# One in sixteen of layer 1's differences on VectorE instead of GpSimd

## What is computed

```
h = relu(layernorm(x));  x = x + layer0(h, adj)     # additive attention over all nodes, 8 heads of 64
h = relu(layernorm(x));  x = x + layer1(h, adj)

def layer1(h, adj):
    keys, queries, values = h @ Wk[head], h @ Wq[head], h @ Wv[head]      # 8 heads of 64
    atts = queries @ keys.T / 8 - 1e16 * (1 - max(adj, eye))
    return sum over heads of softmax(atts) @ values @ Wo[head]
```

## Time and profile before

| | before |
|---|---|
| median of 3 runs | 4598.18 us (4594.34 to 4601.94) |
| the profiled execution | 4598.45 us |
| span of its trace | 4596.6 us |
| busy, share of the span | TensorE 94%, VectorE 80%, GpSimd 75%, ScalarE 71% |
| mean granted clock of TensorE | 0.976 of full |
| DMA | 646.10 MB, mean 141 GB/s |

### The profile page before, as it was taken

How to read it: one execution, slowest core, us unless ns; L and a number is a source line. 1 busy time by engine, 2 the same in 40 slices (tenths; PEclk the granted TensorE clock), 3 DMA queues, 4 the chain that set the end, 5 groups by cost and what they waited for, 6 DMA issues and landing times. The chain is left out here.

```text
span 4596.6 us, 111803 instructions
## 1 busy us (share of the span) xinstructions
PE 4336.9 (94%) x42445; PEld 2092.0 (46%) x42956; DVE 3684.9 (80%) x7790; ACT 3250.4 (71%) x6022; POOL 3426.1 (75%) x2955
## 2 busy tenths in 40 slices
PE   8699999999999979969999999999999999999998
PEld 4222222222222224425665656656656566566565
DVE  5498998988989863358888888878888888888786
ACT  5366666666666643317888878888878788888886
POOL 2476676676767730018998989989989899899897
PEclk9899999999999989979999999999999999999999
DMA  4566676666666533362343433433433334334333
GB/s 145 136 212 195 204 216 211 212 206 212 221 188 204 151 126 115 115 193 75 105 123 88 123 98 96 135 107 98 120 105 113 106 89 127 110 99 129 98 111 104
DMA packets 462939, 646.10 MB, mean 141 GB/s; under 512 B 49536, under 2 KB 271104, under 8 KB 452288
## 3 DMA queue, kind: packets, MB, share of 16 engines
q1 hardware_dynamic: 383968, 522.36, 37.1%
q10 hardware_dynamic: 73856, 100.83, 7.7%
q0 software_dynamic: 4576, 15.73, 1.2%
HBM read 528.38 MB, written 110.38 MB: 139 GB/s over the span
## 5 line engine op out<-in xcount | busy, mean ns | idle before, releaser
L1406 POOL TENSOR_TENSOR d_PL<-d_PF,d_PH 128x512 f16<-128x512 f32 x2048 | 2316.1, 1170 | 234.9 <-ACT d_PH L1456 230.6
L1496 DVE CUSTOM_DVE_ANT_0 d_junk<-d_gd,d_MR 128x512 bf16<-128x512 f32 x2112 | 1438.7, 687 | 412.0 <-issue 342.3
L1452 ACT ACTIVATE d_PF<-d_sc 128x512 f32<-128x512 f32 x2048 | 1253.8, 612 | 445.9 <-DVE d_sc L1585 297.3
L813 DVE SCALAR_TENSOR_TENSOR b_P<-R,u,b_A 128x512 f32<-128x512 f32 x1792 | 1195.2, 738 | 110.8 <-PE b_den L871 68.5
L1456 ACT ACTIVATE d_PH<-d_sc 128x512 f16<-128x512 f32 x2048 | 1262.3, 616 | 0.0
L864 PE MATMUL b_acc<-b_P,V 128*64 128x512 f32 x4096 | 965.4, 610 | 76.0 <-DVE b_P L813 38.4
L1624 PE MATMUL d_gd<-d_KA,d_QA 128*128 128x512 f16 x2112 | 816.1, 387 | 74.3 <-DMA d_KA<-scratch_kl 30.2
L1640 PE MATMUL d_sc<-d_QA,d_KA 128*128 128x512 f16 x2048 | 777.1, 379 | 13.9 <-ACT d_PH L1456 5.4
L1641 PE MATMUL d_sc<-d_QL,d_KB 128*128 128x512 f16 x2048 | 776.6, 379 | 0.0
L1661 PE MATMUL d_acc<-d_V,d_PH 128*128 128x65 f16 x8192 | 639.5, 193 | 2.7 <-ACT d_PH L1456 0.2
L1663 PE MATMUL d_acc<-d_V,d_PH 128*128 128x64 f16 x8192 | 640.3, 193 | 0.0
(11 more groups left out here) (133 smaller groups left out, 4075.8 us busy)
## 6 DMA issues: line engine op xcount, KB each, us to landing
d_V<-scratch_v SPq DMA_DIRECT2D x131, 520.0 KB, 4.2
stage<-in_adjT SPq DMA_DIRECT2D x128, 512.0 KB, 5.2
b_srow<-in_adj ACTq DMA_DIRECT2D x256, 256.0 KB, 4.3
b_rows<-in_adj SPq DMA_DIRECT2D x112, 512.0 KB, 6.4
d_MR<-scratch_mr SPq DMA_DIRECT2D x36, 1024.0 KB, 6.3
d_MT<-scratch_mt SPq DMA_DIRECT2D x35, 1024.0 KB, 6.3
d_KA<-scratch_kh SPq DMA_DIRECT2D x272, 128.0 KB, 3.0
d_KA<-scratch_kl SPq DMA_DIRECT2D x272, 128.0 KB, 3.2
```

Source lines behind the costliest of these rows:

```text
L813: nc.vector.scalar_tensor_tensor(out=PT[:, m % P_STEPS, h, :], in0=R[:, par, h, :], scalar=T["u"][:, m, h:h + 1], in1=A[m % A_RING][:, :], ...
L1406: eng.tensor_tensor(PL[:, t % H_RING, :], PF[:, t % F_RING, :], PH[:, t % H_RING, :], ALU.subtract).then_inc(s_lowp if by_pool(t) else s_l ...
L1452: nc.scalar.activation(PF[:, t % F_RING, :], sc[(nb * TILES + t) % BANKS][:, :], ACT.Exp, scale=EXP_SCALE)
L1496: nc.vector.tensor_tensor_reduce(out=junk[:, gi % 2, :], in0=gd[gi % 2][:, :], in1=MR[:, s, c * QB:(c + 1) * QB], scale=1.0, scalar=-3.0e3 ...
```

## The change

`by_pool(t)` is now true for all tiles but those with t % 16 == 2. These, 16 in a block and 128 in all, are subtracted by VectorE, in the place in its order that `body` has for them: at the start of the step after the tile's own, after `finish` and ahead of the step's first guard. In a pass they are the tiles of steps 1, 9, 17 and 25, so VectorE does them in steps 2, 10, 18 and 26. The slots of `PF` and the engines no longer go together, so the waits are written by tile: ScalarE, before tile t, waits for the difference of tile t - 4 on the engine that makes it, and TensorE for that of tile t. The first values of the two semaphores are 0 instead of the ring's shares.

```diff
-    POOL_SLOTS = (0, 1, 2, 3)
-    PER_RING = (F_RING - len(POOL_SLOTS), len(POOL_SLOTS))
-    SPLITS = tuple(n * TILES // F_RING for n in PER_RING)
...
     def by_pool(t):
-        return t % F_RING in POOL_SLOTS
+        return t % 16 != 2
+
+    SPLITS = tuple(sum(by_pool(t) == own for t in range(TILES)) for own in (False, True))
...
+    def splits_done(nb, t):
+
+        return nb * SPLITS[by_pool(t)] + split_count(t)
...
-            pool.sem_inc(s_lowp, PER_RING[1])
...
-                            act.wait_ge(s_lowp if by_pool(t) else s_low, nb * SPLITS[by_pool(t)] + split_count(t))
+                            if t >= F_RING:
+                                act.wait_ge(s_lowp if by_pool(t - F_RING) else s_low, splits_done(nb, t - F_RING))
+                            elif not first:
+                                before = t - F_RING + TILES
+                                act.wait_ge(s_lowp if by_pool(before) else s_low, splits_done(nb - 1, before))
...
-            if PER_RING[0]:
-                dve.sem_inc(s_low, PER_RING[0])
...
-                    own = by_pool(t)
-                    pe.wait_ge(s_lowp if own else s_low, nb * SPLITS[own] + (PER_RING[own] + split_count(t)))
+                    pe.wait_ge(s_lowp if by_pool(t) else s_low, splits_done(nb, t))
```

## The result

| | before | after |
|---|---|---|
| median (7 runs each) | 4598.70 us (4594.34 to 4604.85) | 4611.87 us (4607.34 to 4613.38) |
| ratio, 95% interval | | 1.0024 [1.0014, 1.0035] |
| profiled execution, its span | 4598.45, 4596.6 | 4609.6, 4607.7 |

A forecast was written before the change was run, and what follows sets the result against it. The prediction took TensorE to set the pace, with GpSimd next. Its terms, 3.0 + 3.8 + 6.4 = 13.2 us, added to 4598 gave 4611 us, 0.28% slower, range 4588 to 4626 (the forecast's own 4607 to 4618).

The forecast's parts named there:

- TensorE sets the pace, GpSimd's relief is worth nothing: Layer 1's attention: TensorE busy 294.6 of 300 us, so taking 128 instructions off GpSimd gains about nothing.
- Rival D: GpSimd was the limit after all and 6% less of its work counts: 4553 us; chance 0.02.
- The bare price of a split: One difference on VectorE, without a wait for GpSimd, delays its next instruction by 0.61 us.
- Steps 10, 18 and 26: Three of four splits in a pass: VectorE's delay is absorbed, cost 0 for 96 splits.
- Rival C's full form: A GpSimd difference has just begun at every split, shutting VectorE out, in steps 10, 18, 26 too: 4706 us; C's chance 0.14.
- The 0.24 of margin: Step 26: VectorE's second guard would return at 2993.54, the guard matmul needing it is at 2993.78.
- Step 2, first pass: VectorE's queue is full; the split, less the division's regained wait, costs TensorE 0.43 us in 7 blocks: 3.0 us.
- Step 2, other passes: Split adds about 0.58, division returns about 0.15; 0.16 us beyond the margin reaches TensorE in 24 passes: 3.8 us.
- The scaling: L1503, 8 columns after a pass's guards, waits 0.20 us longer for GpSimd in all 32 passes: 6.4 us.
- Rival A: The scaling L1503 comes before GpSimd's difference and wins its port: 4591 us, or 4585 with step 2 absorbed; chance 0.17.
- The waits: The edited semaphore waits of ScalarE and TensorE cost nothing, each being for the same tile's difference as before.
- The form of rival C with a few events: VectorE passed over by several differences, at least 3.1 us each; three to six more give 4620 to 4630; C's chance 0.14.

The follow-up runs named there:

- steps_10_18: The changed kernel with only the differences of steps 10 and 18 (64) on VectorE: 4602.82 us, 1.0007 to the kernel before.
- steps_26_27: The changed kernel's split moved to the differences of steps 26 and 27 (64) on VectorE: 4631.42 us, 1.0068 to the kernel before.
- waits_only: The changed kernel's new waits alone, all 2048 differences back on GpSimd: 4599.94 us, 1.0003 to the kernel before.
- step_2: The changed kernel with only the differences of step 2 (32) on VectorE: 4606.68 us, 1.0017 to the kernel before.
- no_scale_after: The changed kernel with the scaling of the 8 columns taken out, its factor put into the guards' reduction: 4597.91 us, 1.0000 to the kernel before.
- step_26: The changed kernel with only the differences of step 26 (32) on VectorE: 4606.62 us, 1.0017 to the kernel before.
- no_scale: The kernel before with the scaling of the 8 columns taken out, its factor put into the guards' reduction: 4633.03 us, 1.0072 to the kernel before.

## Why the prediction held, point by point

- **TensorE sets the pace, GpSimd's relief is worth nothing.** Right. GpSimd lost 18.7 us of work in the 300 of the stretch and TensorE gained none of it. Rival D is out.
- **The bare price of a split, 0.61 to the next start.** Right: 2998.17 to 2998.78. Minimum and median 678 and 686 ns, so 0.07 more in the record, as before.
- **Steps 10, 18 and 26 cost 0 for their splits.** Right: all 96 without a wait, and steps_10_18 level with before. Rival C's full form is out. The 0.24 of margin held.
- **Step 2, first pass: 0.43 in 7 blocks, 3.0 us.** 0.446 on TensorE, 3.1 us. The split's wait (0.93 in all) and the division's gain of 0.33 are where they were put: 1.05 became 0.72.
- **Step 2, other passes: 0.16 in 24, 3.8 us.** 0.19, 0.20 and 0.15: 4.3 us. (By its own numbers the prediction's term is 0.43 - 0.26 = 0.17, 4.1 us.) That it came so near is partly luck. The division was to give back 0.15 everywhere; it gave back 0.12 and 0.11 in second and third passes and nothing in fourth ones, where it took 0.70 before and 0.72 after. What made up for it was not taken apart.
- **The scaling: 0.20 in 32, 6.4 us.** 0.158 to 0.165, 5.1 us. The mechanism was right and the size a quarter too large. The step that failed is the arrival: I let the GpSimd series move with the mask by all of 0.20, and put L1503 0.10 behind a start; it came 0.13 to 0.16 behind one in 30 of the 32 passes, so that 0.17 was the shift. Rival A, in which it wins, did not come: in two passes it took 0.17 us, in one before. In steps_26_27, with two splits moved, it was 29 of 32.
- **The waits cost nothing.** Right, waits_only.
- **Shut-outs as likely after as before.** This step failed. All 33 shut-outs of ten profiles happened where GpSimd's next difference was ready behind the running one. That is so at all 31 divisions of the kernel before and at none of the kernel after, step_2 and no_scale_after, the three with step 2's split on VectorE; those have none. So in its profile the change had taken away what all shut-outs have in common. In the seven profiles where a next one is ready, the count is 1 before, none in waits_only, steps_10_18 and step_26, and 9, 11 and 12 in three whose edits touch neither the division nor the differences beside it. The form of rival C with a few events therefore came in my experiments and not in the change. The price that the prediction names, 3.1 at least, is that of TensorE's idle time alone and leaves out the clock: the steps at the earlier trace rows took 4.7 more.

The sum by terms is 3.1 + 4.3 + 5.1 = 12.5 where I had 13.2, and the medians are 13.2 apart. That the last two agree to a tenth is luck: one term was too large and two too small, the profile before has a shut-out of 4.7 us that the profile after lacks, and the interval is 10 us wide.

What stays open is which division is shut out when a next difference is ready. Over the ten profiles, those that got in behind the running difference had come 0.62 to 1.05 us after its start, and three of them at 0.06 to 0.13; those shut out had come at 0.07 to 0.10, 0.62 to 0.67, 0.86 and 0.95 to 1.03. The two sets overlap, so the arrival alone doesn't decide; what does wasn't found. That a missing next difference protects the division fits all 93 cases but was not made the subject of an edit. Whether the change itself would gain with the reciprocals in PSUM was not tried.

## What to carry to other kernels

When two engines share a port, the price of one more instruction is its bare time plus where in the other engine's instruction it arrives; both can be read from the kernel before, to some hundredths of a us, and each then needs following to the engine that sets the pace, because most of it is absorbed (here 96 of 128). Before moving anything in time near such an instruction, take one of its two SBUF operands to PSUM if it is small: the three edits that should have gained 12 us or more lost 25 to 34 until this was done, and then gained 10 to 23. A wait of the engine that sets the pace can cost more than its own length, so look at the granted clock behind it. And a longest duration that is five times the median deserves an experiment, not a place among the things left out.

## What the hardware did that was not expected

- A tensor_tensor of VectorE with two SBUF inputs isn't only held until GpSimd's running instruction ends: it can be passed over by all that GpSimd has ready behind it, up to three in these runs, and then takes 3.9 to 4.4 us. It happened only where a next difference was ready. In the same kernels others waited for the running one only, and took 0.7 to 1.1. The Trainium skill (SBUF — State Buffer, Who interferes with whom) has the loser block while the other instruction holds the port; the long cases show more than that.
- Where it takes its turn, it starts about 0.14 before the record of GpSimd's instruction ends, and the record of GpSimd's next one, if that follows at once, is 1.60 to 1.64 instead of 1.16.
- After TensorE had sat idle 2.6 to 3.1 us, its granted clock fell to 0.50 in 21 of 33 cases, and such a case cost about 1 us more than one without.
- Even 8 columns of a tensor_scalar with one SBUF input wait so: 174 ns free, 0.89 or 1.05 us behind a difference. A reduction to the same 8 columns never did (219 to 221 ns in all 33 of no_scale, most of them 0.12 to 0.13 after a difference's start, where the scaling waits 0.88). The Trainium skill (SBUF — State Buffer, Who interferes with whom) has `tensor_scalar` among those that can take the shared ports and `tensor_reduce` on this chip never; the rows agree.
